# A three-layer attention and expert kernel: padding, loads and a small exponential are moved to other places

## What is computed

```
x = x + A(layernorm(x))          # cumulative-sum mixer, swiglu
x = x + F(layernorm(x))          # two layers: f0 and f1
x = x + B(layernorm(x))          # full attention, 16 heads of 8
x = x + F(layernorm(x))          # the same two layers: g0 and g1

F, for l in (0, 1):
    x = x + causal_attention(ln(x)) @ wo + bo        # 16 heads of 8
    h = ln(x)
    logits = h @ gate_w + gate_b                     # l = 0: of each token; l = 1: of the mean of h
    vals, idx = top_k(logits, 2);  w = softmax(vals)
    x = x + sum over the two chosen experts of w * (gelu(h @ w1[e] + b1[e]) @ w2[e] + b2[e])
```

## Time and profile before

| | |
|---|---|
| median of 3 runs | 3318.35 us (3314.36 to 3318.41) |
| profiled execution | 3311.18 us |
| its span in the profile | 3309.4 us |
| TensorE (PE) busy | 2676.8 us, 81% |
| VectorE (DVE) busy | 2563.4 us, 77% |
| ScalarE (ACT) busy | 2275.7 us, 69% |
| GpSimd (POOL) busy | 568.4 us, 17% |
| causal attention f0, searches to last values | about 188 to 590 us |

### The profile page before, as it was taken

The page is one execution under the profiler, slowest core; times in us unless marked ns, Lnnn a source line. Parts: engine busy times, 40 slices in busy tenths (PEclk is TensorE's granted clock), DMA queues, the critical chain, the costliest instruction groups (busy, mean ns, idle before and its releaser), DMA issues. The chain is left out here.

```text
span 3309.4 us, 71725 instructions
## 1 busy us (share of the span) xinstructions
PE 2676.8 (81%) x28144; PEld 1186.6 (36%) x28144; DVE 2563.4 (77%) x3323; ACT 2275.7 (69%) x4368; POOL 568.4 (17%) x1096
## 2 busy tenths in 40 slices
PE   3459999699499994749999999289996996699976
PEld 3322332487233332512222222233332784223325
DVE  5659998477499993769999996489994675699956
ACT  1137898377278984439999999158885674488965
POOL 3033110244131101000000000132101442221001
PEclk8669999699599996869999999689998898799988
DMA  1060000221500001130000000510001213300010
GB/s 31 5 146 27 13 10 10 60 59 42 127 21 14 12 10 45 50 80 8 10 8 8 10 8 10 136 37 15 12 10 41 61 49 78 77 16 12 10 36 26
DMA packets 105438, 119.05 MB, mean 36 GB/s; under 512 B 15063, under 2 KB 83213, under 8 KB 105101
## 3 DMA queue, kind: packets, MB, share of 16 engines
q1 hardware_dynamic: 96460, 96.63, 10.4%
q0 software_dynamic: 4480, 13.90, 2.0%
q10 hardware_dynamic: 4160, 3.93, 0.6%
HBM read 70.31 MB, written 43.78 MB: 34 GB/s over the span
## 5 line engine op out<-in xcount | busy, mean ns | idle before, releaser
L1201 ACT ACTIVATE h_probsf<-h_ps_scoresf 128x512 f32<-128x512 f32 (+3 forms) x1216 | 603.6, 552 | 182.3 <-PE h_ps_scoresf L1151 169.9
L1201 ACT ACTIVATE h_probsg<-h_ps_scoresg 128x512 f32<-128x512 f32 (+3 forms) x1216 | 603.5, 552 | 174.5 <-PE h_ps_scoresg L1151 162.0
L1201 ACT ACTIVATE h_probsb<-h_ps_scoresb 128x512 f32<-128x512 f32 x1024 | 556.3, 596 | 94.3 <-PE h_ps_scoresb L1151 84.3
L1173 PE MATMUL h_ps_valuesf<-h_probsf,v_all 128*9 128x256 f32 (+2 forms) x4608 | 352.1, 378 | 29.1 <-POOL h_probsf L1264 22.3
L1173 PE MATMUL h_ps_valuesg<-h_probsg,v_all 128*9 128x256 f32 (+2 forms) x4608 | 348.1, 374 | 26.0 <-POOL h_probsg L1264 18.6
L1173 PE MATMUL h_ps_valuesb<-h_probsb,v_all 128*9 128x256 f32 x4096 | 318.0, 382 | 9.4 <-ACT h_drainedb L1208 4.9
L1225 DVE TENSOR_REDUCE h_maxima_0b<-h_ps_scanb 128x2 f32<-128x1024 f32 x256 | 292.4, 1216 | 30.9 <-POOL h_maxima_2b L1256 21.5
L1225 DVE TENSOR_REDUCE h_maxima_2b<-h_ps_scanb 128x2 f32<-128x1024 f32 x256 | 292.8, 1216 | 6.7 <-PE h_ps_scanb L1113 6.7
L1113 PE MATMUL h_ps_scanf<-k_stack,q_stack 48*128 48x512 bf16 (+3 forms) x1280 | 218.4, 364 | 74.7 <-DVE h_maxima_0f L1232 47.1
L1225 DVE TENSOR_REDUCE h_maxima_0f<-h_ps_scanf 128x2 f32<-128x1024 f32 x224 | 259.3, 1219 | 23.0 <-PE h_ps_scanf L1113 22.8
L1113 PE MATMUL h_ps_scang<-k_stack,q_stack 48*128 48x512 bf16 (+3 forms) x1280 | 217.2, 361 | 73.8 <-DVE h_maxima_0g L1232 47.3
(11 more groups left out here) (406 smaller groups left out, 4324.3 us busy)
## 6 DMA issues: line engine op xcount, KB each, us to landing
q_stack<-combine_weights SPq DMA_DIRECT2D x64, 256.0 KB, 3.2
q_stack<-in_L_ffn_e_w SPq DMA_DIRECT2D x24, 256.0 KB, 2.8
q_stack<-q_parts SPq DMA_DIRECT2D x20, 256.0 KB, 4.0
k_stack<-k_parts SPq DMA_DIRECT2D x20, 256.0 KB, 8.2
attended<-h_drainedf SPq DMA_DIRECT2D x16, 256.0 KB, 2.2
attended<-h_drainedf SPq DMA_DIRECT2D x32, 128.0 KB, 1.9
attended<-h_drainedb SPq DMA_DIRECT2D x32, 128.0 KB, 1.9
attended<-h_drainedg SPq DMA_DIRECT2D x16, 256.0 KB, 2.2
```

The source lines that it names most:

```text
L1173: last = nc.tensor.matmul(ps_values[32 * j:32 * j + VD, low:high], m.v_all[:, kb, QUAD * quad + j, :], probs[:, (u + j % banks) % RING_P, ...
L1201: nc.scalar.activation(by_head(probs[:, of % RING_P, :], of), by_head(ps_scores[:, of % RING_S, :], of), ACT.Exp, scale=SOFTMAX_SCALE).the ...
```

## The change

Three things change.

1. The fills of the maxima tiles go from the start of `attention_heads` into `project_qkv`, on GpSimd ahead of its load of chunk 1 (`buffers.pad`). Their semaphore gets a phase of its own, so that the later clearing finds it.
2. Only chunks 0 and 1 (`EARLY = 2`) are loaded by SyncE and GpSimd inside `project_qkv`. The loads of chunks 2 and 3 go into `attention_heads`. In causal layers SyncE issues those of chunk 2 behind the first shift and those of chunk 3 behind the second; GpSimd issues its halves ahead of masks 0 and 4. In the full attention both queues issue them at once, ahead of everything.
3. The exponential is computed by GpSimd as e to the power d, from a tile filled with e: in layer 0 after the split of the fourth expert's w2, in layer 1 ahead of the splits. Both Exp activations go from ScalarE's list.

```diff
@@ set_up, gpsimd
+            nc.gpsimd.memset(m.euler[:, :], math.e)
...
+EARLY = 2
...
@@ project_qkv
-            for c in range(1, CHUNKS):
-                load_stacks(pool, c, 1)
+            buffers.pad(nc, m)
+            load_stacks(pool, 1, 1)
 
         @block.sync
...
-                    if c and part == 0:
+                    if part == 0 and 0 < c <= EARLY:
                         load_stacks(sp, c - 1, 0)
-            load_stacks(sp, CHUNKS - 1, 0)
...
@@ AttentionBuffers
+    def pad(self, nc, m):
+        padded = m.phase_semaphores("pads")("h_padded")
+        for x in self.layouts:
+            nc.gpsimd.memset(self.maxima[x][:, :, :, :], MASKED).then_inc(padded, 1)
...
@@ attention_heads, gpsimd
-            for x in layouts:
-                nc.gpsimd.memset(maxima[x][:, :, :, :], MASKED).then_inc(padded, 1)
             if load_experts:
                 weights = ExpertWeights(nc, m, pool, raw_weights)
+            if not causal:
+                for c in range(EARLY, CHUNKS):
+                    projected["load"](pool, c, 1)
             for k, u in enumerate(on_diagonal):
+                if k % 4 == 0 and k // 4 < CHUNKS - EARLY:
+                    projected["load"](pool, EARLY + k // 4, 1)
...
@@ attention_heads, sync
-            for kind, g in plan.moves:
+            if not causal:
+                for c in range(EARLY, CHUNKS):
+                    projected["load"](sp, c, 0)
+            for k, (kind, g) in enumerate(plan.moves):
                 (shift if kind == "shift" else write)(g)
+                if causal and k < CHUNKS - EARLY:
+                    projected["load"](sp, EARLY + k, 0)
...
@@ experts, gpsimd
+            def exponential():
+                pool.wait_ge(top_ready, 1)
+                nc.gpsimd.tensor_tensor(t["ed"][:, :, 0], m.euler[0:t["d"].shape[0], 0:t["d"].shape[1]], t["d"][:, :, 0],
+                                        ALU.pow).then_inc(exp_ready, 1)
+
             if by_token:
                 pool.wait_ge(hn_ready, CHUNKS)
+            else:
+                exponential()
             for e in range(n_exp):
+                if by_token and e == 4:
+                    exponential()
...
@@ experts, scalar
-                act.wait_ge(top_ready, 1)
-                nc.scalar.activation(t["ed"], t["d"], ACT.Exp).then_inc(exp_ready, 1)
                 act.wait_ge(bias_in, 16 * 2 * TOPK)
...
-                if by_token and k == 5:
-                    act.wait_ge(top_ready, 1)
-                    nc.scalar.activation(t["ed"], t["d"], ACT.Exp).then_inc(exp_ready, 1)
```

More of the change, by code:

```diff
@@ L1 @@
+import math
 import numpy as np
@@ L117, in __init__ @@
         self.neg_half = sb("neg_half", [P, TILES])
+        self.euler = sb("euler", [P, TILES])
         self.vecs = sb("vecs", [P, N_VEC])
@@ L572, in _, with project_qkv @@
                     nc.scalar.activation(g_t[:, :], turned_in(gate), ACT.Copy).then_inc(ug_copied, 1)
-def project_qkv(nc, m, n, first=None, layer=None):
+EARLY = 2
+def project_qkv(nc, m, n, buffers, first=None, layer=None):
     mixing = layer is None
@@ L785, in project_qkv @@
     return {"h": (h_ready, CHUNKS), "high": (high_ready, 2 * CHUNKS), "rest": (rest_ready, 2 * CHUNKS),
-            "v": (v_kept, CHUNKS)}
+            "v": (v_kept, CHUNKS), "load": load_stacks}
 SCAN_KEYS = 512
@@ L1081, in attention_heads @@
         drained, cleared, hidden = sem("h_drained_"), sem("h_cleared"), sem("h_hidden")
-        padded = sem("h_padded")
+        padded = m.named["h_padded"]
         shift_in = [sem(f"h_shift_in{k}") for k in range(2)]
@@ L1319, in _ @@
                 pool.wait_ge(added, CHUNKS)
-                m.clear(pool, "project", "attention")
+                m.clear(pool, "project", "pads", "attention")
         @block.sync
@@ L1499, in _ @@
                 if y == CLEAR_AT:
-                    m.clear(pool, "project", "attention", "finish")
+                    m.clear(pool, "project", "pads", "attention", "finish")
                 if e == 0 and c >= 2:
@@ L1847, in layer @@
         buffers = AttentionBuffers(nc, ctx, n, not mixing, load_experts)
-        projected = project_qkv(nc, m, n, first=first, layer=number)
+        projected = project_qkv(nc, m, n, buffers, first=first, layer=number)
         attention_heads(nc, m, n, buffers, projected)
```

## The result

| | before | after |
|---|---|---|
| median | 3316.36 us (4 runs) | 3236.14 us (3231.26 to 3240.05, 4 runs) |
| ratio | | 0.9761 (95%: 0.974 to 0.9783) |
| profiled execution | 3311.18 us | 3240.05 us |
| TensorE busy | 81% | 83% |
| VectorE busy | 77% | 79% |

The forecast was 3234.4. The total held; which part of the change earns it, and what it costs on the way, is another matter, and the experiments are mostly about that. One thing first: by the ratio the change is worth 79 us, while the two profiled executions lie only 71.1 apart. A later profile of the same changed kernel (changed_again) had a span 7.2 us shorter. Between these two profiles a single attention differs by up to 3.8 us and the layer-0 experts of f0 and g0 together by 5.0.

The account below looks back on a forecast made before the run. Causal attentions were taken to wait for GpSimd's fills, held behind its loads. 81.9 − 3.2 − 2.0 + 2.5 + 4.8 = 84.0 us off 3311.18, plus 7.2 to the median, gave 3234.4; range 3220 to 3262.

Parts of the forecast that it names:

- Fills (a): Causal attentions: fills ahead of GpSimd's loads let VectorE's first reductions start earlier, all that follows moving along; gain 81.9 us.
- Shifts (b): Causal attentions: moved shifts go out while DMAs are busy and land slightly late, 0.8 us a layer; loss 3.2 us.
- the rival with −20.4: Causal attentions: shifts take as long as the large DMAs around them, losing 20.4 us, time 3251.6; chance 0.20.
- its bytes are few and the ring has some 5 us since the last write's issue: Causal attentions, first shift: reason for taking 0.8 us lost a layer, within bounds of 0 and 4.
- Masks (c): Causal attentions: GpSimd's issues of chunk 3 between masks 4 and 5 delay values, 0.5 us a layer; loss 2.0 us.
- Full attention (d): Full attention: chunk 3's writes no longer wait behind chunk 2's loads, so its k arrives sooner; gain 2.5 us.
- The sign of being wrong that the prediction named: Full attention: chunk 3 of k still 22 us behind chunk 2's issue would show the prediction wrong.
- Exponential (e): Layer-0 experts: the exponential as GpSimd's power lets TensorE turn weights 2.4 us sooner a layer; gain 4.8 us.
- The "may be more" in the text: Layer-0 experts: choice steps might quicken while GpSimd stands still, making the gain 2.8 us instead of 2.4.
- The table loads: Layer-0 experts, ScalarE: two table loads of 1.28 us go, but ScalarE is not what TensorE waits for.
- Layer 1 (f): Layer-1 exponential of one number: GpSimd's power takes 0.6 us and is there in time; gain nothing, bounds 0 and −1.6.
- the 7.2 us that were added to reach the median: Whole kernel: the median of the runs shown lay 7.17 us above the profiled execution, so 7.2 was added to 3227.2.

Follow-up runs that it names:

- pads_only: The kernel before with the fills of the maxima moved ahead of GpSimd's loads, and nothing else: 3296.79 us, ratio 0.9953.
- loads_later: The changed kernel with causal loads of chunk 2 behind the second shift, chunk 3 behind the fourth move (GpSimd's ahead of masks 8 and 16): 3232.71 us, ratio 0.9764.
- load_before_shift: The changed kernel with SyncE's loads of chunk 2 ahead of the first shift, chunk 3 behind the second: 3249.53 us, ratio 0.981.
- full_again: Repeat run: changed kernel, in the full attention k of all chunks loaded first, q of chunks 1 to 3 behind the first moves: 3217.32 us, ratio 0.9713.
- one_early: The changed kernel with only chunk 0 loaded ahead of a causal attention, chunks 1 to 3 later (GpSimd's ahead of masks 4, 16, 32): 3236.11 us, ratio 0.978.

## Why the prediction was right, and where it wasn't

**Fills (a), 81.9.** The size held: the reductions start 79.9 us sooner. The step said the fills earn it by going ahead of the loads, and that "the whole of what follows" hangs on these reductions and "moves ahead with them". pads_only refutes that as a statement on part 1: 15.5 us. What follows hangs on the shift as well, which was behind the same loads on SyncE. The number came out because part 2 cleared both.

**Shifts (b), −3.2, and the rival with −20.4.** This term failed in size. In three of four layers the first shift took 9.0, 8.3 and 7.4 us to the scores instead of 4.1, 12.4 in all, and in f0 the second took 9.5 instead of 7.5. The last drains lost 12.9 of the 79.9, where (b) and (c) together allowed 5.2. So the shifts were caught, as the rival had it, in three layers of four. Its price is not shown: in loads_later, with no first shift late, 80.4 us at the reductions are 70.8 at the last drains, and 9.6 are lost all the same. The step that went wrong is "its bytes are few and the ring has some 5 us since the last write's issue": it looked at SyncE's queue only. What stands in the way is GpSimd's load of chunk 2, released by the same landing of writes and issued 0.8 to 1.2 us ahead of the shift in f1, g0 and g1. In f0 it was issued 1.3 us behind the shift, and the shift took its 4.1 us. load_before_shift and loads_later move only such issues and get 12.5 and 4.1 us in f0, 10.2 and 4.1 in f1. How near is near can be read from full_again, whose causal layers are those of the changed kernel. In its f0 the shift was issued at 195.83, 0.4 us ahead of GpSimd's load, and took 6.8 us:

```profile
196.26 1.14 POOL L643 DMA_DIRECT2D q_stack<-q_parts  x2 [9.62 <-DMA q_parts<-p_partsf]
...
202.36 0.61 PE L1164 MATMUL h_ps_scoresf<-q_stack,k_stack 49*128 49x512 bf16 x2 [2.53 <-DMA q_stack<-h_shiftsf]
```

The Trainium skill has this in "DMA: Bandwidth & Descriptors", section "Queues, rings and completion order", by which a semaphore increment of a DMA engine lands behind all of its earlier writes, whichever queue they came from. The trace agrees as far as it goes: 4.1 us behind nothing, 7.4 to 9.0 behind a load issued earlier on GpSimd's queue, and 9.5 for f0's second shift behind loads of both queues. It does not tell the order of the increments from a DMA engine that is merely full, and the 6.8 us of a shift issued ahead of the load show that the order of issue on two queues is not all there is. The prediction cited the rule and gave its rival 0.20. GpSimd's loads of chunk 2 were in the trace before, 1.4 us ahead of the shift's new place at 196.2 and beside SyncE's of 194.57; that was the thing to look at:

```profile
194.84 1.11 POOL L635 DMA_DIRECT2D q_stack<-q_parts  x2 [8.72 <-DMA q_parts<-p_partsf]
```

**Masks (c), −2.0.** In f0, GpSimd's issues of chunk 3 (203.79 to 206.01) delayed six masks and no visible wait of TensorE followed; its waits for masks were 20.1 us in f and 18.5 in g, and 22.3 and 18.6 before: 0. one_early shows where such a step does bite, next to a split: 3.35 us.

**Full attention (d), +2.5.** 0.7 in the stage, 0.6 at the scan of chunk 3. The issue of chunk 3's loads did move, from 56.6 to 48.3 us into the stage, but the DMAs were then full to the end. The step reckoned 4.2 MB at 215 GB/s, the rate of f0's stretch; they moved 187 GB/s over 21.1 us, 3.9 MB. In the same stretch before, from 1417.5 to 1439.65, they had moved 178 GB/s at a share of 0.82. Taking away the pause in front of a full pipe gave back only what the pipe had idled. The sign of being wrong that the prediction named, chunk 3 of k 22 us behind chunk 2's issue, all but came (21.1).

**Exponential (e), +4.8.** 2.4 and 2.5 us in the two profiled stages, 5.4 and 4.4 in those of changed_again at a higher clock; and by another way. Timeline of the changed f0:

```profile
621.30 0.18 DVE L1403 TENSOR_TENSOR q_stack<-q_stack 128x16 f32<-128x16 f32 x1
...
621.55 2.91 POOL L1509 TENSOR_TENSOR q_stack<-euler,q_stack 128x16 f32<-128x16 f32 x1 [10.40 <-DVE q_stack L1403]
...
624.41 0.61 POOL L1521 CAST e_w_hif<-q_stack 128x512 fp32r<-128x512 f32 x1
...
625.66 0.77 DVE L1410 TENSOR_SCALAR q_stack<-q_stack 128x16 f32<-128x16 f32 x1
...
627.13 1.31 DVE L1413 TENSOR_TENSOR q_stack<-q_stack 128x128 f32<-128x128 f32 x1
628.47 0.29 DVE L1414 TENSOR_TENSOR q_stack<-q_stack 128x128 f32<-128x128 f32 x1
...
628.82 1.02 PE L1720 MATMUL e_ps_turnf<-ident,q_stack 128*8 128x128 f32 x4 [2.42 <-DVE q_stack L1414]
```

The power took 2.91 us (2.93 said). But from the end of the choice to TensorE's turn it is 7.3 us, against 6.9 before: `combine` needed 3.1 us from 625.66 instead of 1.4, because GpSimd's delayed splits now run beside it (L1413 1.31 us, L1414 0.29), and it started 1.2 us behind the power, behind a split of VectorE's own. What was gained is the choice, 4.1 us instead of 6.1, in which GpSimd stands still; TensorE's pause fell from 3.67 to 2.42, and its turn came 1.3 us sooner into the stage (37.0 and 38.3). What made the rest of the 2.4 is not shown. The "may be more" in the text was the real gain, and the gain that it named was eaten. The table loads are gone, and as the prediction said they are not what TensorE waited for.

**Layer 1 (f), 0.** The power of one number took 0.54 us (0.6 said), and VectorE went on 0.86 us after its start, where it was 0.90 with the exponential.

**Sum.** 79.9 for the reductions, less 12.9, plus 0.7 and 4.9 are 72.6, next to the 71.1 of the two profiled executions. For changed_again the same sum is 66.0 at the last drains, 1.0 and 9.9, 76.9 next to the 78.3 of the spans. So most of what lies between 71 and 79 is in the layer-0 experts and goes with the granted clock there (0.92 and 0.94 in f0), for which the forecast had no term; single executions of one kernel scatter by some 9 us.

The forecast's closeness (1.7 us) is partly luck. The gain was forecast as 84.0 and is 79: (b) and (c) allowed 5.2 us where 12.9 were lost, (a) and (d) were 2 us too good each, and the experts gave 4.9 and 9.9 us in the two profiles where (e) had 4.8. And the 7.2 us that were added to reach the median of three runs are no property of the kernel: 35 later runs of it had medians of 3311.1 to 3311.5, like the profiled execution, and the changed kernel again had 3232.3. Some 5 us of gain too many met a start that was 7 us too high.

## What to carry to other kernels

When an operation waits behind DMA issues in a queue's order, ask for everything that stands behind the same issues: the fill was one, the shift the other, and moving the fill alone gave 15 us of 79. A small DMA on which an engine waits has to be issued ahead of bulk loads on every queue, not only on its own, and here by about a microsecond. Freeing it is worth only what the next shift, the masks and the clock don't take back: look at the whole layer. Where the DMAs are full, order the bytes by need: k before q was worth 13 us in one stage and 15 in the time, where three other placings of the causal loads were worth nothing that shows.

## What the runs showed of the hardware

- Two DMAs of 2 KB took 4.1 us from computed to used with no load near. They took 7.4 to 9.0 us if GpSimd's loads had been issued 0.8 to 1.2 us earlier on their own queue, and 7.8 to 10.0 us from their issue behind SyncE's (load_before_shift). Issued ahead of such loads by 1.3 us they took 4.1, by 0.4 us 6.8 (full_again, f0).
- VectorE's step on 128x128 floats in SBUF took 0.29 us, and 1.25 to 1.32 us when it started within 0.3 us after one of GpSimd's subtractions (L1494, L1523, 1.3 us each). The slow steps ended 0.15 us after the subtraction; a step on 128x16 took 0.77 instead of 0.17 and ended with it. Beside GpSimd's casts (L1492) the reductions kept their 0.29. A pause of GpSimd's subtractions shortens VectorE's chain beside it.
- GpSimd's power of e cost 2.91 us for 16 columns and 0.54 for one; the power of the variances in the earlier trace rows cost 2.93 for 16 columns.
- In loads_later's f1 TensorE paused for 1.35 us ahead of 880.97. Its scores of 512 columns took 0.39 us there and 0.61 from 882.05 on; the granted clock of 879.7 to 889.7 was 0.66, a mean of the low and the high level (0.50 and 1.00).
